# Attention scores with the row maximum set in the score banks by ScalarE, in place of a row product on TensorE

## The chip, the cores and the metric

The kernel runs on one core of one Trainium2 chip. The metric is the device time of one execution in microseconds, taken as the median over runs. The profile is of one further execution.

## What is computed

Two sequences of 1024 tokens with 128 features go through one block: a conditioned layer norm, attention with 16 heads of 64 features whose queries and keys come from latents of 64, a gated residual, a second conditioned norm, and a mixture of 8 experts with a gated residual. The change is in the attention:

```
q = rope((c_q @ w_up_q.T) split in heads);  k = rope((c_kv @ w_up_k.T) split in heads)
scores = einsum('bhqd,bhkd->bhqk', q, k) * scale
attn = softmax(scores, axis=-1)
out = einsum('bhqk,bhkd->bhqd', attn, v) @ w_out.T + residual
```

Softmax takes the maximum of each query's row away from its scores before the exponential.

## The kernel before

**Tiles and loops.** Heads are taken in pairs, 8 pairs a sequence, 16 in all (p = 0 to 15). Both heads of a pair work side by side, one on partitions 0 to 63 and one on 64 to 127. A pair has 16 steps (st): two halves of 512 queries, and in each half 8 tiles of 128 keys (kt = st % 8). A step computes the scores of 128 keys against 512 queries, keys on partitions, for both heads: 128x1024 numbers in two of the four banks of `ps_s` (even steps banks 0 and 1, odd steps banks 2 and 3). Scores are needed nearly exactly, so they are made of three products of rounded parts, upper by upper, lower by upper, upper by lower (L440, L442, L444), two matmuls each, one a head. A fourth product (L446) multiplies a stationary row of ones with `neg_row`, one row that holds minus the maximum of every query, and so takes the maximum away in PSUM. Then ScalarE writes the exponential to `probs` (L697), TensorE multiplies it with the values into `ps_o` (`pv`, L456), and GpSimd adds it up for the denominators (`add`, L939).

**The maxima.** They belong to queries, and queries have to lie on partitions to be reduced. So the same scores are computed once more, roughly and the other way round, one pair ahead: `maxima` (L422) puts 128 queries against 512 keys of both heads into `ps_m`, VectorE reduces them (`reduce_max`, L1097), and `neg_max` (L1102) makes minus the maximum of half a pair's queries, 8 numbers on each of 128 partitions (`nm`). `max_rows` (L1384) turns that into rows by 8 DMAs from SBUF to SBUF, each of 128 runs of 4 bytes. There is one `ps_m` for all: each use by TensorE waits until VectorE has reduced the one before.

**The order of the work.** It is written out by hand, in groups of two steps (g = 0 to 7). In a group of pair p, TensorE issues one maxima product of pair p+1, the scores of steps 2g and 2g+1, a second maxima product, one up projection of pair p+2 (`up`, L410), and the value steps 2g-2 and 2g-1. In groups 3 and 7 it also multiplies the denominators of half a pair (L464) into bank 2 and the output of half a pair (L473) into bank 3 of `ps_s`, after waiting for the group's exponentials; this is why the scores of steps 1 and 9 wait for `den_read` and `out_added`. Each up projection takes both halves of `ps_x`: VectorE turns it (`turn`, L1079 to L1084), ScalarE takes the upper bits (`upper`, L689), VectorE the lower bits (`lower`, L1090), and the next projection waits for that last one:

```
                elif q >= 2:
                    pe.wait_ge(s["lower"], n_unit(q, u) - 1)
```

VectorE's order in a group is: at the beginning of groups 0 and 4 the addition of the outputs to x (L1153); the first reduction; `lower` of the projection of the group before; the second reduction; in groups 3 and 7 `neg_max`; `turn`; in groups 0 and 4 the reciprocals of denominators (L1139), in groups 2 and 6 the division of the latent sums by them (L1144). ScalarE's order is: in groups 0 and 4 the copy of the denominators (`den_out`, L709); `upper` (L689); the two exponentials; in groups 0 and 4 the copy of the latent sums (L704).

**SyncE's queue**, in each pair: the second half's maxima of this pair; the denominators of a half as columns (`den_cols`, L1392), after their reciprocal back to HBM as rows (`inv_rows`, L1397) and from there spread over partitions (`inv_spread`, L1402); the first half's maxima of the next pair; the same three for the other half; the weights of pair p+4 (L1374). SyncE waits in this order, so each waits for those ahead.

The last pair has no maxima and no projections beside it, pair 14 no projections. There VectorE also normalises the first sequence and routes its tokens. Before the pairs come norms, latents and the maxima of pair 0, after them the experts.

## Time and profile before

| | |
|---|---|
| median of 3 runs | 900.91 us (897.12 to 901.8) |
| profiled execution | 895.69 us |
| its span, first to last instruction | 894.0 us |
| mean granted TensorE clock | 0.963 of full speed |
| TensorE matmuls busy | 813.2 us (91%), 5118 instructions |
| TensorE weight loads busy | 485.9 us (54%) |
| VectorE busy | 637.1 us (71%) |
| GpSimd busy | 662.7 us (74%) |
| ScalarE busy | 397.2 us (44%) |
| time on the chain that ended last | PE 82%, DVE 8%, DMA 4%, POOL 2% |

PE is TensorE's matmuls and PEld its weight loads, which run beside them; DVE is VectorE, ACT ScalarE, POOL GpSimd, SP SyncE. A matmul's recorded duration holds its way through the array, so neighbouring ones overlap: a busy share says that something was in flight, not that the engine could take no more. L numbers are lines of the kernel before. The chain of waits is followed back from the last instruction, at each step to what released it, or to the instruction before it on its engine.

### The profile page before, as it was taken

What the parts mean: (1) busy time and instruction counts of PE and PEld (TensorE: products, weight loads), DVE (VectorE), ACT (ScalarE), POOL (GpSimd) and SP (SyncE); (2) the same over time, 40 slices, a digit from 0 to 9 for tenths busy, and PEclk for the clock granted to TensorE, in tenths of its full rate; (3) what the DMA queues carried; (4) which work ended last, traced back from release to release, by engine and by line L of the source; (5) the groups of instructions that cost most, each with busy time, mean ns of one, the idle gap of its engine ahead of it and who ended that gap; (6) DMA issues with size and microseconds to landing.
All of it is one profiled execution on the core that took longest, in us unless ns stands there. A gap on an engine that the chain in (4) does not pass through costs nothing.

```text
span 894.0 us, 14690 instructions
## 1 busy us (share of the span) xinstructions
PE 813.2 (91%) x5118; PEld 485.9 (54%) x5118; DVE 637.1 (71%) x1156; ACT 397.2 (44%) x650; POOL 662.7 (74%) x348
## 2 busy tenths in 40 slices
PE   4689999999999999999999999999999977968581
PEld 2445555555555555555555555555555444368581
DVE  8987777777777777777777777777776757646022
ACT  3654444444444444444444444444444433336340
POOL 2579998898987878787878787878777856632333
PEclk8979999999999999999999999999999999969796
DMA  9101001010101011111011111101010000078683
GB/s 246 31 1 14 13 14 25 14 25 13 25 13 26 13 26 14 27 20 26 6 26 25 22 25 14 24 14 14 13 13 15 12 13 1 19 238 269 213 314 89
DMA packets 84330, 43.91 MB, mean 49 GB/s; under 512 B 57632, under 2 KB 73376, under 8 KB 84192
## 3 DMA queue, kind: packets, MB, share of 16 engines
q1 hardware_dynamic: 83232, 40.86, 18.2%
q0 software_dynamic: 1024, 2.10, 0.7%
q8 instruction: 42, 0.69, 0.3%
q14 instruction: 32, 0.26, 0.1%
HBM read 36.51 MB, written 6.16 MB: 48 GB/s over the span
## 4 chain that ended last, share of the span: by engine, by line
PE 82%; DVE 8%; DMA 4%; POOL 2%; issue 2%; ACT 1%; POOLq 0%; SPq 0%; DVEq 0%
PE ps_o L456 25%; PE ps_m L422 9%; PE ps_x L410 8%; PE ps_s L440 7%; PE ps_s L442 6%; PE ps_s L446 6%; PE ps_s L444 6%; PE ps_s L473 3%; DMA moe<-xs_dram 3%; PE ps_s L464 3%; PE ps_s L595 2%; PE ps_s L586 2%; POOL xs_dram L953 2%; DVE mx L1097 1%; PE ps_s L377 1%
## 5 line engine op out<-in xcount | busy, mean ns | idle before, releaser
L939 POOL TENSOR_TENSOR acc<-acc,probs 128x1024 f32<-128x1024 f32 (+1 forms) x192 | 459.9, 2395 | 74.7 <-ACT probs L697 52.5
L1097 DVE TENSOR_REDUCE mx<-ps_m 128x2 f32<-128x1024 f32 x240 | 293.7, 1224 | 90.9 <-PE ps_m L422 90.3
L697 ACT ACTIVATE probs<-ps_s 128x1024 f32<-128x1024 f32 x256 | 248.8, 1024 | 157.7 <-PE ps_s L446 157.6
L456 PE MATMUL ps_o<-probs,c_all 128*64 128x512 f32 x1024 | 249.5, 608 | 0.0
L440 PE MATMUL ps_s<-q_hi,k_hi 64*128 64x512 f32 x512 | 102.6, 397 | 12.0 <-DVE x_sb L1153 12.0
L456 PEld LDWEIGHTS ps_o<-probs,c_all 128*64 128x64 f32 x1024 | 62.4, 136 | 93.2 <-issue 44.5
L422 PE MATMUL ps_m<-k_hi,q_hi 64*128 64x512 f32 x480 | 107.7, 444 | 4.0 <-DVE mx L1097 4.0
L939 POOL TENSOR_TENSOR acc<-probs 128x1024 f32<-128x1024 f32 (+1 forms) x32 | 75.4, 2357 | 48.3 <-ACT probs L697 47.8
L442 PE MATMUL ps_s<-q_hi,k_lo 64*128 64x512 f32 x512 | 101.4, 391 | 0.0
L446 PE MATMUL ps_s<-neg_row,one_row 64*128 64x512 f32 x512 | 101.3, 391 | 0.0
L444 PE MATMUL ps_s<-q_lo,k_hi 64*128 64x512 f32 x512 | 100.8, 389 | 0.0
L422 PEld LDWEIGHTS ps_m<-k_hi,q_hi 64*128 64x128 f32 x480 | 46.0, 183 | 91.4 <-issue 81.3
L440 PEld LDWEIGHTS ps_s<-q_hi,k_hi 64*128 64x128 f32 x512 | 48.7, 186 | 24.0 <-issue 17.0
L1153 DVE TENSOR_TENSOR x_sb<-x_sb,ps_s 128x512 f32<-128x512 f32 x30 | 20.6, 685 | 49.9 <-PE ps_s L473 49.9
L444 PEld LDWEIGHTS ps_s<-q_lo,k_hi 64*128 64x128 f32 x512 | 48.7, 186 | 10.8
L446 PEld LDWEIGHTS ps_s<-neg_row,one_row 64*128 64x128 f32 x512 | 48.6, 185 | 10.8
L442 PEld LDWEIGHTS ps_s<-q_hi,k_lo 64*128 64x128 f32 x512 | 48.7, 186 | 10.5
L709 ACT COPY den<-ps_s 128x512 f32<-128x512 f32 x30 | 17.6, 585 | 77.9 <-PE ps_s L464 77.9
L1084 DVE TENSOR_TENSOR ps_x<-ps_x,tmp 128x256 f32<-128x256 f32 x112 | 48.4, 433 | 3.8
L689 ACT CAST q_hi<-ps_x 128x256 fp32r<-128x256 f32 x56 | 20.9, 374 | 66.8 <-DVE ps_x L1084 66.8
L1079 DVE TENSOR_TENSOR ps_x<-ps_x,rot 128x256 f32<-128x256 f32 x112 | 47.3, 422 | 0.0
L1082 DVE TENSOR_TENSOR tmp<-ps_x,rot 128x256 f32<-128x256 f32 (+1 forms) x113 | 47.1, 417 | 0.0
(299 smaller groups left out, 1025.5 us busy)
## 6 DMA issues: line engine op xcount, KB each, us to landing
probs<-in_experts SPq DMA_DIRECT2D x15, 578.0 KB, 6.0
rr<-rd_dram SPq DMA_DIRECT2D x62, 128.0 KB, 3.1
wu<-in_wqk SPq DMA_DIRECT2D x16, 256.0 KB, 3.4
neg_row<-nm SPq DMA_DIRECT2D x256, 0.5 KB, 2.0
w_first<-in_experts SPq DMA_DIRECT2D x5, 578.0 KB, 5.2
rot<-in_experts SPq DMA_DIRECT2D x5, 578.0 KB, 5.0
hT<-in_experts SPq DMA_DIRECT2D x5, 578.0 KB, 5.6
xs_dram<-zero SPq DMA_DIRECT2D x2, 960.0 KB, 9.4
```

What stands on the lines that cost most here:

```text
L410: ins = nc.tensor.matmul(bank, m[:, q % 2, w, twin, :], src, start=(n == 0), stop=(n == 1))
L422: ins = nc.tensor.matmul(bank[:, h, :], q_hi[rows(h), q % 3, qt * P:(qt + 1) * P], k_hi[rows(h), q % 3, kh * HALF:(kh + 1) * HALF], start= ...
L440: nc.tensor.matmul(bank[h], k_hi[rows(h), p % 3, kc], q_hi[rows(h), p % 3, qc], start=True, stop=False)
L442: nc.tensor.matmul(bank[h], k_lo[rows(h), p % 3, kc], q_hi[rows(h), p % 3, qc], start=False, stop=False)
L444: nc.tensor.matmul(bank[h], k_hi[rows(h), p % 3, kc], q_lo[rows(h), p % 3, qc], start=False, stop=False)
L446: ins = nc.tensor.matmul(bank[h], one_row[rows(h), :], neg_row[rows(h), p % 2, qc], start=False, stop=True)
L456: ins = nc.tensor.matmul(ps_o[64 * h:64 * h + 64, :], c_all[:, (p // HP) * TB + kt, :], probs[:, st % 4, h, :], start=(kt == 0), stop=(kt ...
L697: nc.scalar.activation(probs[:, st % 4, :, :], ps_s[:, 2 * (st % 2):2 * (st % 2) + 2, :], ACT.Exp, scale=SCALE).then_inc(s["probs"], 1)
L939: V.tensor_tensor(acc[:, half, heads, :], first, probs[:, st % 4, heads, :], ALU.add).then_inc(s["added"], 1)
L1079: V.tensor_tensor(straight, straight, cos_sb[:, c], ALU.mult).then_inc(s["turned"], 1)
L1084: V.tensor_tensor(straight, straight, part, ALU.add).then_inc(s["rotated"], 1)
L1097: V.reduce_max(mx[:, :, kh, qt], max_banks(q, n), AX.X).then_inc(s["max_reduced"], 1)
```

## The change

ScalarE copies minus the maxima, which now lie on all 128 partitions (`neg_wide`), into a step's two score banks before the scores come (`preset`), and TensorE adds the three products to what the banks hold. The fourth product, its row of ones and its row of maxima are gone. The score matmuls wait for `preset` alone. What they waited for before (the exponentials of the step two back, the maxima's landing, `den_read` and `out_added`) `preset` now waits for on ScalarE; at steps 1 and 9 it works in two pieces, bank 2 after `den_read`, bank 3 after `out_added`. In ScalarE's order the presets of the next two steps come behind the exponentials of a group, those of steps 1 and 9 behind `den_out`. The matmuls of `outputs` form one accumulation group over their bank instead of four. On TensorE value step 2g-1 moves behind the denominators and outputs.

The maxima go from `nm` to HBM by one DMA a half pair, 1024 runs of 4 bytes, and from there by two DMAs (one a head, 256 KB each) to all partitions; the two stages wait for each other. In SyncE's order they come last in each half pair, behind the inverses. The buffer is single: the spread waits until the last preset of the same half of the pair before has read it.

```
-        one_row = sb("one_row", [P, P], F32R)
-        neg_row = sb("neg_row", [P, 2, S], F32R)
+        neg_wide = sb("neg_wide", [P, 2, 2, HALF])
...
-        nm = sb("nm", [P, 2, 2, 4], F32R)
+        nm = sb("nm", [P, 2, 2, 4])
...
+        mr_dram = nc.dram_tensor("mr_dram", [2, 2, HALF], F32, kind="Internal").ap()
...
@@ -428,22 +430,15 @@
                 half, kt = divmod(st, TB)
                 if st == 0:
                     pe.wait_ge(*lowers(p))
-                ge(pe, s["probs"], n_step(p, st) - 2)
-                if kt == 0:
-                    pe.wait_ge(row_placed[half], 128 * (p + 1))
-                if kt == 1:
-                    ge(pe, s["den_read"], n_part(p, half) - 2)
-                    ge(pe, s["out_added"], n_part(p, half) - 3)
+                pe.wait_ge(s["preset"], n_step(p, st))
                 kc, qc = slice(kt * P, (kt + 1) * P), slice(half * HALF, (half + 1) * HALF)
                 bank = [ps_s[:, 2 * (st % 2) + h, :] for h in range(2)]
                 for h in range(2):
-                    nc.tensor.matmul(bank[h], k_hi[rows(h), p % 3, kc], q_hi[rows(h), p % 3, qc], start=True, stop=False)
+                    nc.tensor.matmul(bank[h], k_hi[rows(h), p % 3, kc], q_hi[rows(h), p % 3, qc], start=False, stop=False, skip_group_check=True)
                 for h in range(2):
-                    nc.tensor.matmul(bank[h], k_lo[rows(h), p % 3, kc], q_hi[rows(h), p % 3, qc], start=False, stop=False)
+                    nc.tensor.matmul(bank[h], k_lo[rows(h), p % 3, kc], q_hi[rows(h), p % 3, qc], start=False, stop=False, skip_group_check=True)
                 for h in range(2):
-                    nc.tensor.matmul(bank[h], k_hi[rows(h), p % 3, kc], q_lo[rows(h), p % 3, qc], start=False, stop=False)
-                for h in range(2):
-                    ins = nc.tensor.matmul(bank[h], one_row[rows(h), :], neg_row[rows(h), p % 2, qc], start=False, stop=True)
+                    ins = nc.tensor.matmul(bank[h], k_hi[rows(h), p % 3, kc], q_lo[rows(h), p % 3, qc], start=False, stop=True, skip_group_check=True)
                 ins.then_inc(s["scores"], 1)
...
-                                           g_all[:, p // HP, p % HP, :], start=True, stop=True)
+                                           g_all[:, p // HP, p % HP, :], start=(n == 0), stop=(n == 3))
...
-                    for n in (2 * g - 2, 2 * g - 1):
+                    def value_step(n):
                         if n >= 0:
                             pv(p, n)
                         elif p > 0:
                             pv(p - 1, NSTEP + n)
+
+                    value_step(2 * g - 2)
                     if g in (3, 7):
                         pe.wait_ge(s["probs"], n_step(p, 2 * g + 1))
                     if g == 3 and p > 0:
@@ -564,6 +561,7 @@
                         outputs(p - 1, 0, ps_s[:, 3, :])
                     if g == 7 and p > 0:
                         outputs(p - 1, 1, ps_s[:, 3, :])
+                    value_step(2 * g - 1)
...
+
+            def preset(p, st):
+
+                half, kt = divmod(st, TB)
+                if p == 0 and st < 2:
+                    act.wait_ge(s["max_reduced"], NMAX - 1 + st)
+                ge(act, s["probs"], n_step(p, st) - 2)
+                if kt == 0:
+                    act.wait_ge(row_wide[half], 32 * (p + 1))
+                if kt == 1 and (p or half):
+                    ge(act, s["den_read"], n_part(p, half) - 2)
+                    nc.scalar.copy(ps_s[:, 2, :], neg_wide[:, half, 0, :])
+                    ge(act, s["out_added"], n_part(p, half) - 3)
+                    nc.scalar.copy(ps_s[:, 3, :], neg_wide[:, half, 1, :]).then_inc(s["preset"], 1)
+                else:
+                    nc.scalar.copy(ps_s[:, 2 * (st % 2):2 * (st % 2) + 2, :], neg_wide[:, half, :, :]).then_inc(s["preset"], 1)
...
+            preset(0, 0)
+            preset(0, 1)
             for p in range(NPAIR):
                 for g in range(NGRP):
                     if g == 0 and p > 0:
                         den_out(p - 1, 0, ps_s[:, 2, :])
+                        preset(p, 1)
                     if g == 4 and p > 0:
                         den_out(p - 1, 1, ps_s[:, 2, :])
+                    if g == 4:
+                        preset(p, 9)
                     if g == 6 and p == LAST:
...
                     expo(p, 2 * g)
                     expo(p, 2 * g + 1)
+                    if g < NGRP - 1:
+                        preset(p, 2 * g + 2)
+                        if g != 3:
+                            preset(p, 2 * g + 3)
+                    elif p < LAST:
+                        preset(p + 1, 0)
...
-            V.memset(ones[:], 1.0)
-            V.memset(one_row[:].bitcast(F32), 0.0)
-            then(V.memset(neg_row[:].bitcast(F32), 0.0))
-            V.memset(one_row[0:1, :].bitcast(F32), 1.0)
-            V.memset(one_row[64:65, :].bitcast(F32), 1.0).then_inc(s["constants"], 1)
+            V.memset(ones[:], 1.0).then_inc(s["constants"], 1)
...
             def neg_max(q, half):
                 dve.wait_ge(s["max_reduced"], NMAX * q + TB * (half + 1))
-                ge(dve, row_placed[half], 128 * q)
+                ge(dve, row_out[half], 16 * q)
...
             def max_rows(q, half):
 
                 sp.wait_ge(s["max_row"], 2 * q + half + 1)
-                if q >= 2:
-                    sp.wait_ge(s["scores"], n_step(q - 2, TB * half + TB - 1))
+                sp.dma_start(mr_dram[half].rearrange("h (t p) -> p h t", p=P), nm[:, half, :, :],
+                             allow_slow_non_contiguous=True).then_inc(row_out[half], 16)
+
+            def max_spread(q, half):
+
+                sp.wait_ge(row_out[half], 16 * (q + 1))
+                if q:
+                    sp.wait_ge(s["preset"], n_step(q - 1, TB * half + TB - 1))
                 for h in range(2):
-                    for n in range(4):
-                        row = neg_row[64 * h:64 * h + 1, q % 2, half * HALF + n * P:half * HALF + (n + 1) * P]
-                        sp.dma_start(row.bitcast(F32), nm[:, half, h, n:n + 1].bitcast(F32)).then_inc(row_placed[half], 16)
+                    sp.dma_start(neg_wide[:, half, h, :],
+                                 mr_dram[half, h:h + 1, :].to_broadcast([P, HALF])).then_inc(row_wide[half], 16)
...
-            sp.wait_ge(s["constants"], 1)
-            max_rows(0, 0)
-            max_rows(0, 1)
+            for half in range(2):
+                max_rows(0, half)
+                max_spread(0, half)
             weights(3)
 
             for p in range(NPAIR):
                 if p > 0:
-                    if p < LAST + 1:
-                        max_rows(p, 1)
                     den_cols(p - 1, 0)
                     inv_rows(p - 1, 0)
                     inv_spread(p - 1, 0)
-                if p < LAST:
-                    max_rows(p + 1, 0)
+                    max_rows(p, 1)
+                    max_spread(p, 1)
                 if p > 0:
                     den_cols(p - 1, 1)
                     inv_rows(p - 1, 1)
                     inv_spread(p - 1, 1)
+                if p < LAST:
+                    max_rows(p + 1, 0)
+                    max_spread(p + 1, 0)
                 if p + 4 <= LAST:
                     weights(p + 4)
```

## Rows read from the trace of the kernel before

**Rows 1.** Busy time by stretch: stretch, its length, then each engine's busy us, TensorE's clock, DMA.

```profile
65.30:680.10 614.80, 614.01 (x3892) 349.79 (x3892) 472.20 (x777) 285.57 (x391) 523.59 (x232) 1.00 0.11 18
680.10:722.90 42.80, 39.95 (x251) 21.03 (x250) 32.71 (x45) 17.99 (x20) 34.55 (x16) 1.00 0.08 14
```

**Rows 2.** Chain of waits, 65.3 to 680.1: shares by line, then one piece.

```profile
by line: PE ps_o L456 33.7%; PE ps_m L422 12.1%; PE ps_x L410 12.1%; PE ps_s L440 8.4%; PE ps_s L442 8.4%; PE ps_s L446 8.4%; PE ps_s L444 8.3%; PE ps_s L473 4.6%; PE ps_s L464 3.8%; DVE mx L1097 0.2%; issue 0.0%
...
317.92 1.87 PE ps_o L456 x8
```

**Rows 3.** Timeline of weight loads, 314.6 to 327: start, length, and idle time before.

```profile
314.69 0.19 PEld L422 LDWEIGHTS ps_m<-k_hi,q_hi 64*128 64x128 f32 x2 [0.81 <-issue]
...
317.18 0.19 PEld L410 LDWEIGHTS ps_x<-cq,wh 128*128 128x128 f32 x1 [0.35 <-DVE q_lo L1090]
...
319.72 0.19 PEld L422 LDWEIGHTS ps_m<-k_hi,q_hi 64*128 64x128 f32 x2 [0.81 <-issue]
...
326.69 0.19 PEld L422 LDWEIGHTS ps_m<-k_hi,q_hi 64*128 64x128 f32 x2
```

**Rows 4.** Timeline of VectorE, 314.7 to 327.5.

```profile
315.24 1.23 DVE L1097 TENSOR_REDUCE mx<-ps_m 128x2 f32<-128x1024 f32 x1 [0.61 <-PE ps_m L422]
316.38 0.41 DVE L1090 TENSOR_TENSOR q_lo<-ps_x,q_hi 128x256 fp32r<-128x256 f32 x1
...
319.56 0.68 DVE L1144 TENSOR_TENSOR ou<-ou,rr 128x512 f32<-128x512 f32 x1
...
327.40 1.22 DVE L1097 TENSOR_REDUCE mx<-ps_m 128x2 f32<-128x1024 f32 x1
```

**Rows 5.** Timelines of VectorE and weight loads where TensorE waits, near 113.

```profile
112.70 0.41 DVE L1090 TENSOR_TENSOR k_lo<-ps_x,k_hi 128x256 fp32r<-128x256 f32 x1
...
113.36 0.19 PEld L410 LDWEIGHTS ps_x<-ck,wh 128*128 128x128 f32 x1 [0.24 <-DVE k_lo L1090]
```

**Rows 6.** ScalarE: timeline, and one group of instructions with busy us and mean ns.

```profile
314.66 0.37 ACT L689 CAST q_hi<-ps_x 128x256 fp32r<-128x256 f32 x1 [1.61 <-DVE ps_x L1084]
316.17 1.94 ACT L697 ACTIVATE probs<-ps_s 128x1024 f32<-128x1024 f32 x2 [1.14 <-PE ps_s L446]
...
325.72 0.58 ACT L709 COPY den<-ps_s 128x512 f32<-128x512 f32 x1 [2.59 <-PE ps_s L464]
...
L727 ACT CAST q_hi<-acc 128x512 fp32r<-128x512 f32 x1 | 0.6, 617 | 0.0
```

**Rows 7.** Timelines of GpSimd's additions and VectorE's divisions.

```profile
317.27 2.37 POOL L939 TENSOR_TENSOR acc<-acc,probs 128x1024 f32<-128x1024 f32 x1
...
319.78 2.72 POOL L939 TENSOR_TENSOR acc<-acc,probs 128x1024 f32<-128x1024 f32 x1
...
692.11 2.37 POOL L939 TENSOR_TENSOR acc<-acc,probs 128x1024 f32<-128x1024 f32 x1
...
692.62 2.41 DVE L1144 TENSOR_TENSOR ou<-ou,rr 128x512 f32<-128x512 f32 x1
```

**Rows 8.** SyncE: timeline; then DMA issues: count, size of one, median us to landing.

```profile
323.78 5.23 SPq L1384 DMA_DIRECT2D neg_row<-nm  x8
...
rr<-rd_dram SPq DMA_DIRECT2D x62, 128.0 KB, 3.1
...
xs_dram<-zero SPq DMA_DIRECT2D x2, 960.0 KB, 9.4
...
denc<-den SPq DMA_DIRECT2D x62, 2.0 KB, 2.1
...
rd_dram<-rc SPq DMA_DIRECT2D x31, 4.0 KB, 2.1
```

**Rows 9.** Timeline of ScalarE, before the first pair and in the last.

```profile
64.14 1.28 ACT L697 ACT_TABLE_LOAD   x1
...
741.82 1.94 ACT L697 ACTIVATE probs<-ps_s 128x1024 f32<-128x1024 f32 x2 [1.61 <-PE ps_s L446]
745.75 1.95 ACT L697 ACTIVATE probs<-ps_s 128x1024 f32<-128x1024 f32 x2 [1.99 <-PE ps_s L446]
```

More of the change, by code:

```diff
@@ L211, in build @@
             "max_row": "both heads' maxima of half the queries, negated (vector)",
-            "scores": "both heads' scores of a step, less the maximum (tensor)",
+            "preset": "a step's score banks hold minus the maximum (scalar)",
+            "scores": "both heads' scores of a step, added to it (tensor)",
             "probs": "their probabilities (scalar)",
@@ L250, in build @@
         up_in = sem("up_in")
-        row_placed = [sem(f"row_placed{n}") for n in range(2)]
+        row_out = [sem(f"row_out{n}") for n in range(2)]
+        row_wide = [sem(f"row_wide{n}") for n in range(2)]
         den_cols_in, inv_out, inv_in = sem("den_cols_in"), sem("inv_out"), sem("inv_in")
```

## The prediction

> **What bounds the kernel now.** I read the stretches first: 614.8 of the span's 894 us are one regular stage, from 65.3 to 680.1 us, with TensorE busy for 614.0 us at full granted clock, VectorE 472, GpSimd 524 and ScalarE 286 [rows 1]. Then the chain of waits over that stage: it names TensorE for 99.8%, and the row product (L446) for 8.4%, which is 51.6 us, or 0.23 for each of 224 steps [rows 2]. So the ready answer is that a row product taken away shortens the kernel by its own time. Before believing it I asked how late the next engine is, and laid out one group of two steps: TensorE's weight loads, which tell when it was let go [rows 3], beside VectorE's instructions of the same 5 us [rows 4]. The reader should see a loop in them. A group starts with the loads for its first maxima at 314.69. VectorE reduces that product from 315.24 (0.55 later, 1.23 long), then takes a lower half from 316.38 to 316.79, and only then may TensorE start the next up projection, which goes into the bank that this instruction read: 317.18. Projection and two value steps last until the next group's start at 319.72. These stations are in series, whatever the scores between them cost. The loop's only slack is from 316.79 to 317.18, 0.39 us, less the handover itself. How long a handover takes is shown where TensorE really waits: lower half ends 112.70+0.41=113.11, load at 113.36, so 0.25 [rows 5]. Slack: 0.14 us of a group of 5.03. The forecast rests on that number, which neither chain nor busy shares show.
>
> **The change, part by part.**
> Row product: TensorE has 0.46 us less a group, 51.6 over 14 pairs of 8 groups. Off the path comes less. The new group is 0.55 + 1.14 (315.24 to 316.38) + 0.41 + 0.25 = 2.35 to the projection, + 2.54 (317.18 to 319.72) = 4.89, against 5.03: 0.14. The other 0.32 turns into waits of TensorE for the first reduction, ahead of its second maxima, and for the lower half. The granted clock should stay: pair 14, where TensorE is busy 39.95 of 42.8 us, has it at 1.00 [rows 1].
> The Trainium skill, Trainium Kernel Development and Optimization, "Performance Expectations", calls matmul busy time a bad measure of an engine's distance to its limit and weight-load busy time a good one. By that rule TensorE, with loads for 350 us of the 615, would not be the bound and its product worth nothing; by the busy row it would be worth all; the loop lies between, nearer to the rule.
> Groups with denominators and outputs last 326.69-319.72=6.97, 1.94 more [rows 3]. One value step (half of 1.87 [rows 2]) now stands behind the outputs: nothing is added, but VectorE adds the outputs 0.9 us earlier against the next group, where it had held up the reduction (327.40 is 0.71 behind the start, not 0.55 [rows 4]), 0.02 beyond the slack. A half pair was 3 x 5.03 + 6.97 + 0.02 = 22.08 and becomes 4 x 4.89 + 1.94 = 21.50: 0.58 less.
> VectorE's division, once a half pair behind the third group's rotation, waits for GpSimd's addition to end: issued at 319.56, done at 320.24, the addition ending at 317.27+2.37=319.64 [rows 4, 7]. Its end was just in time for the next reduction, due 0.55 behind 319.72. GpSimd takes 2.51 from one addition to the next (317.27 to 319.78), 5.02 a group, more than 4.89: released 2.35 behind the second group (0.23 earlier than now, with the scores), three in a row end at 9.78, that is 4.89 behind the third. The division ends 0.60 later at 5.49, the reduction was due at 4.89+0.55=5.44, and it needs 0.02 more to start: between 0.07 and, with a lengthened addition, 0.11. I take 0.11. Net 0.47 a half pair. Pairs 1 to 13: 26 x 0.47 = 12.2; pair 0, without divisions, 7 x 0.14 = 1.0.
> Presets: 256 copies of 128x1024 new on ScalarE. No row copies from SBUF to PSUM. Below: an Exp of this shape, two in 1.94, so 1.02 alone and 0.92 in a row; above: the SBUF-sourced cast of half the size, 0.617, doubled to 1.23 [rows 6]. I take 1.02/0.92, the row with the same size. ScalarE's group is then 0.37 (upper half) + 1.94 + 1.84 = 4.15, with the upper bound 4.77: under 4.89, so TensorE's group hides it. In time: exponentials ran from 1.48 to 3.42 behind the group's start, now 0.23 earlier, to 3.2; presets end at 4.1 and 5.0, wanted by scores at 5.0 and 5.7. Were that cover gone, each 0.1 us more a preset would cost 0.2 a group.
> At a half pair ScalarE has the denominators' copy (0.58), one bank's preset, a wait for VectorE's output addition, the other bank's preset, and queued behind that wait an upper half and the next exponentials. Outputs are ready 2.35+2.54+1.94-0.94=5.9 behind the fourth group's start, added at 6.85, preset at 7.5; TensorE wants the bank at 7.65 and has 0.3 of idle time above. Zero, with 0.4 of cover.
> Maxima's way: SyncE had 8 small DMAs a half pair (5.2 us of issuing [rows 8]) ahead of the inverses; now 1+2 behind them. From the denominators: two DMAs 2.1+0.6, reciprocal in VectorE's turn (done 5.1 behind the pair's start), inverse rows 2.1, two spreads issued in 1.2, maxima to HBM X, spread of twice the size 1.2+3.7 (3.1 for half of it) [rows 8]: 13.3+X, wanted by the ninth preset at 17.8, harmless until 19.8 by the cover above. X: 2.1 for the inverse rows' write of 256 runs, below; 9.4 for the zero fill's 1920 runs of 512 B, above. I take 3, nearest to the write of small runs. Zero. The weight DMA queued behind has a pair's time; the other half's rows go the same way four groups later.
> Start: two presets and the table load of 1.28, idle time until now [rows 9], get in front of the first exponentials: +0.8. The memsets gone at the beginning lay beside the token DMAs: 0. Pair 14 has no projections and waits for reductions already; earlier output additions: -0.4. Last pair: groups of 3.93 (741.82 to 745.75 [rows 9]) meet ScalarE's 1.94+1.84+0.25=4.03: +0.5; its long waits for VectorE's router stay.
> Sum: -12.2-1.0+0.8-0.4+0.5 = -12.3. The profiled execution took 895.7 (1.7 of it round the span), so 883.4; the shown runs' median is 5.2 above it, so **888.6** for that median.
>
> **Rivals.**
> B, the product was on the path with all its time: 900.9-51.6-0.4=849. For: chain and busy time [rows 1, 2]. Against: 0.25 us of handover [rows 5]; it would have to vanish, and reductions to move with it.
> C, slower: the division falls behind the next addition instead of ahead of it. Where it met a running one it took 2.41, not 0.68: 692.62+2.41=695.03, 0.55 after that addition's end at 694.48 [rows 7]. It decides if GpSimd starts the next addition (5.03 behind the group) before the division is issued (4.75 to 4.87), a margin of 0.2. Then the division ends at 8.0 and the reduction is 2.5 late, 26 times: 900.9-12.3-2.9+65=951. The Trainium skill, SBUF — State Buffer, "Who interferes with whom", makes it a rule: a VectorE instruction with two SBUF inputs and a GpSimd one that reads SBUF exclude each other, and the first to start keeps the ports; by that rule, the trace agrees (2.41 against 0.68).
> D, rows late: 1024 runs of 4 bytes need X above 6.5. At the far bound of 9.4: 2.9 x 26 = 75 more, 900.9-12.3+75=964; break-even at X=7.0. Against: the 256 runs' 2.1. The Trainium skill, DMA: Bandwidth & Descriptors, speaks against such a write in "Rules for kernel authors" (a strided last dimension becomes one descriptor per element) and "Specifications" (below 512 B an engine reads, modifies and writes); it gives no time, and no run here shows such a write to HBM.
> E, ScalarE in the way: presets at 1.23 and the wait for output additions cost half a microsecond a half pair and eat the gain of 12: 898 to 903.
>
> **How the numbers follow.** The forecast's mechanism 0.70, B 0.07, C 0.08, D 0.04, E 0.11. Its own range is 880 to 896: 0.06 of a handover times 112 (7), with runs 5 apart. 8 in 10 lie between 868 (handovers 0.1 cheaper, 11, no delay by divisions, 3, and a fast run) and 904 (E); B is left below, C and D above. Within 0.5% (896.4 to 905.4) is about what a measurement of this kernel cannot tell from no change. Faster: 0.69+0.07=0.76; same: E and the forecast's edge, 0.12; slower: C and D, 0.12.
>
> **What would show it.** Groups of 4.89 between loads for first maxima; TensorE waiting some 0.3 us a group for reductions and lower halves, 112 times, and no longer busy all the stage; divisions still near 0.7; presets near 1.02, the ninth not waiting for rows. Groups of 4.57 mean B, divisions of 2 to 3 us C, a half pair's first preset behind a DMA D, scores waiting for presets E.

## Result: slower by 8%, and the profile after

The changed kernel takes **974.03 us** (median of 4 runs, 967.99 to 986.77) against 899.01 for the kernel before beside it: ratio 1.081, interval 1.074 to 1.088; the ratio leaves out the run of 986.77, a slow one with a granted clock of 0.915 against 0.924 to 0.938. The forecast was 888.6 in a range of 868 to 904. It fell into rival D, rows late, to which I had given 0.04 and a time of 964.

The page of the kernel after, its busy times, its chain, two groups of instructions:

```profile
span 972.6 us, 13807 instructions
...
PE 829.1 (85%) x4606; PEld 451.4 (46%) x4606; DVE 642.9 (66%) x1152; ACT 634.8 (65%) x937; POOL 662.5 (68%) x348
...
DMA 51%; PE 17%; DVE 15%; issue 6%; ACT 5%; SPq 4%; POOL 1%; ACTq 0%; POOLq 0%; DVEq 0%
...
L712 ACT COPY ps_s<-neg_wide 128x1024 f32<-128x1024 f32 x225 | 222.4, 1026 | 136.8 <-DMA neg_wide<-mr_dram 136.8
```

Over its whole span the chain of the kernel before was 82% TensorE's and 4% DMA's (in the regular stage 99.8% TensorE's [rows 2]); the chain of this one is 51% DMA's. The presets last 1.03 us, as bounded, but ScalarE idles 136.8 us ahead of them, for the maxima's rows. The chain of waits of one half pair (start, length, what) shows where these are; SPq is SyncE's queue:

```profile
307.98 7.56 DMA mr_dram<-nm
...
315.94 4.66 DMA neg_wide<-mr_dram
...
320.68 0.04 ACT ps_s L712
```

The write of 1024 neighbouring runs of 4 bytes takes 7.56 us here. Over the whole execution, from the summary of that one line (L1400), it takes from issue to landing:

```profile
DMA to landing us min/median/max: 7.6/9.1/10.3
```

The timelines of ScalarE and of weight loads around it (start, length, the engine's instruction, and in brackets its idle time before):

```profile
320.68 1.02 ACT L712 COPY ps_s<-neg_wide 128x1024 f32<-128x1024 f32 x1 [3.22 <-DMA neg_wide<-mr_dram]
```

```profile
309.40 0.19 PEld L424 LDWEIGHTS ps_m<-k_hi,q_hi 64*128 64x128 f32 x2 [0.81 <-issue]
...
311.75 0.19 PEld L412 LDWEIGHTS ps_x<-cq,wh 128*128 128x128 f32 x1 [0.25 <-DVE k_lo L1111]
...
314.28 0.19 PEld L424 LDWEIGHTS ps_m<-k_hi,q_hi 64*128 64x128 f32 x2 [0.81 <-issue]
```

ScalarE waits 3.22 us for one preset. The half pair with this wait in it, from the outputs at 319.17 to those at 341.76, is 22.59 us long, 0.97 more than the 21.62 of a version without such waits (e13 below); the one ahead of it, with a wait of 4.20, is 23.58, 1.96 more. So some 2.2 us of each wait are covered, near the 2.0 of the forecast. The one behind them, with a wait of 4.26, is 25.16, 3.54 more: over it TensorE is granted 0.93 of its clock, over the other two 1.00. The mean over all half pairs is 24.8. And a group that doesn't meet this wait answers to [rows 3] exactly as forecast: 314.28 - 309.40 = 4.88 us between first maxima, the projection 2.35 behind the start, and TensorE waiting for the lower half with a handover of 0.25. So two things were to be shown: that this write alone cost the time, and that the rest does bring what the loop said.

### The profile page after: what moved, and what is told of

It is laid out like the page before. It is cut to its first block, busy times and chain, and to the rows that moved or that the text cites. A ratio compares the mean times of both kernels' runs of the same rounds, so it can differ in the third digit from the quotient of the medians.

```text
span 972.6 us, 13807 instructions
## 1 busy us (share of the span) xinstructions
PE 829.1 (85%) x4606; PEld 451.4 (46%) x4606; DVE 642.9 (66%) x1152; ACT 634.8 (65%) x937; POOL 662.5 (68%) x348
## 3 DMA queue, kind: packets, MB, share of 16 engines
q0 software_dynamic: 1024, 2.10, 0.7%
## 4 chain that ended last, share of the span: by engine, by line
DMA 51%; PE 17%; DVE 15%; issue 6%; ACT 5%; SPq 4%; POOL 1%; ACTq 0%; POOLq 0%; DVEq 0%
DMA mr_dram<-nm 27%; DMA neg_wide<-mr_dram 12%; DMA rd_dram<-rc 8%; DVE mx L1118 4%; SPq L1428 3%; PE ps_s L437 3%; PE ps_o L451 2%; PE ps_s L441 2%; PE ps_m L424 2%; PE ps_s L439 2%; DMA moe<-xs_dram 2%; ACT ps_s L710 2%; PE ps_s L584 1%; PE ps_s L593 1%; ACT ps_s L712 1%
## 5 line engine op out<-in xcount | busy, mean ns | idle before, releaser
L712 ACT COPY ps_s<-neg_wide 128x1024 f32<-128x1024 f32 x225 | 222.4, 1026 | 136.8 <-DMA neg_wide<-mr_dram 136.8
L695 ACT ACTIVATE probs<-ps_s 128x1024 f32<-128x1024 f32 x256 | 250.4, 1024 | 61.7 <-PE ps_s L441 61.3
L451 PE MATMUL ps_o<-probs,c_all 128*64 128x512 f32 x1024 | 263.2, 625 | 0.0
L437 PE MATMUL ps_s<-q_hi,k_hi 64*128 64x512 f32 x512 | 114.9, 443 | 67.6 <-ACT ps_s L712 43.2
L424 PE MATMUL ps_m<-k_hi,q_hi 64*128 64x512 f32 x480 | 120.4, 492 | 12.3 <-DVE mx L1118 9.6
L441 PE MATMUL ps_s<-q_lo,k_hi 64*128 64x512 f32 x512 | 107.6, 412 | 0.0
L439 PE MATMUL ps_s<-q_hi,k_lo 64*128 64x512 f32 x512 | 107.4, 412 | 0.0
L441 PEld LDWEIGHTS ps_s<-q_lo,k_hi 64*128 64x128 f32 x512 | 52.4, 198 | 11.7
L1111 DVE TENSOR_TENSOR q_lo<-ps_x,q_hi 128x256 fp32r<-128x256 f32 x56 | 23.3, 416 | 28.4 <-ACT q_hi L687 28.3
L468 PEld LDWEIGHTS ps_s<-hT,ou 128*128 128x128 f32 x240 | 29.0, 191 | 24.5 <-issue 23.5
L412 PE MATMUL ps_x<-ck,wh 128*128 128x256 f32 x112 | 39.4, 370 | 0.0
L1111 DVE TENSOR_TENSOR k_lo<-ps_x,k_hi 128x256 fp32r<-128x256 f32 x56 | 23.3, 417 | 24.0 <-ACT k_hi L687 24.0
```

The lines of the kernel that those rows point to most:

```text
L424: ins = nc.tensor.matmul(bank[:, h, :], q_hi[rows(h), q % 3, qt * P:(qt + 1) * P], k_hi[rows(h), q % 3, kh * HALF:(kh + 1) * HALF], start= ...
L437: nc.tensor.matmul(bank[h], k_hi[rows(h), p % 3, kc], q_hi[rows(h), p % 3, qc], start=False, stop=False, skip_group_check=True)
L439: nc.tensor.matmul(bank[h], k_lo[rows(h), p % 3, kc], q_hi[rows(h), p % 3, qc], start=False, stop=False, skip_group_check=True)
L441: ins = nc.tensor.matmul(bank[h], k_hi[rows(h), p % 3, kc], q_lo[rows(h), p % 3, qc], start=False, stop=True, skip_group_check=True)
L451: ins = nc.tensor.matmul(ps_o[64 * h:64 * h + 64, :], c_all[:, (p // HP) * TB + kt, :], probs[:, st % 4, h, :], start=(kt == 0), stop=(kt ...
L695: nc.scalar.activation(probs[:, st % 4, :, :], ps_s[:, 2 * (st % 2):2 * (st % 2) + 2, :], ACT.Exp, scale=SCALE).then_inc(s["probs"], 1)
```

## Experiments

**Two ways to make the write harmless, first try.** One writes runs of 16 bytes and turns them round in the preset's read:

```diff
-mr_dram[half].rearrange("h (t p) -> p h t", p=P), nm[:, half, :, :]
+mr_dram[half].rearrange("h (p t) -> p h t", p=P), nm[:, half, :, :]
...
-nc.scalar.copy(ps_s[:, 2, :], neg_wide[:, half, 0, :])
+nc.scalar.copy(ps_s[:, 2, :].rearrange("q (t p) -> q t p", p=P), neg_wide[:, half, 0, :].rearrange("q (p t) -> q t p", p=P))
...
```

The copies of the other presets are turned the same way.

> After, with the maxima written to HBM as 256 runs of 16 bytes instead of 1024 of 4; the preset's copy reads them in turned order. Theory W (the write of 1024 short runs, 9.1 us median, is what made the change slower; all else of the forecast holds): the write lands in 2.2 to 2.9 like the inverse rows' 256 runs, the ninth and first presets no longer wait for their rows, groups stay 4.89, half pairs fall from about 25 to 21.6, the time is 885 to 892. Rival S (the two stages through HBM, with 256 KB spreads last in SyncE's queue, are too long as such): the write is short but presets still wait over 1 us a half pair; 900 to 930. Rival A (ScalarE, with 640 us of work and its waits, is the limit): waits move to TensorE for presets; 900 or more. A preset over 1.1 us would mean that the turned read costs.

Measured: 1005.7 us, ratio 1.121 (1.117 to 1.125). The write lands 2.9 us after its issue (median), no preset waits for rows, and yet it is slower still:

```profile
L712 ACT COPY ps_s<-neg_wide 128x1024 f32<-128x1024 f32 x225 | 454.3, 2065 | 0.0
...
L695 ACT ACTIVATE probs<-ps_s 128x1024 f32<-128x1024 f32 x256 | 253.9, 1056 | 4.1 <-PE ps_s L441 3.5
```

A copy that reads every fourth word takes 2.07 us instead of 1.03, and ScalarE, idle 0 and 4.1 us ahead of its two large groups, has become the bound. The run shows that the write can be had cheaply; what the rest of the change is worth it could not show.

The other keeps the 4-byte runs and issues the write first in a half pair's DMAs, its spread last:

```diff
 if p > 0:
+    max_rows(p, 1)
     den_cols(p - 1, 0)
     inv_rows(p - 1, 0)
     inv_spread(p - 1, 0)
-    max_rows(p, 1)
     max_spread(p, 1)
+if p < LAST:
+    max_rows(p + 1, 0)
...
```

> After, with 1024 runs of 4 bytes kept, but the write issued first in each half pair and only its spread last. Theory W with the DMA engines' rings in common: the write still takes 7 to 9 us, but lands before the spread is due; if the small denominators' DMAs issued behind it land in 2 us as ever, the time is that of the 16-byte version, 885 to 892. If they have to wait behind it (landing in 5 us or more), VectorE stands at its reciprocal at the end of groups 0 and 4, and the time lies between, 900 to 950. Rival S: no gain against after, about 974, since the spread is last all the same.

Measured: 965.7 us (one run), 8 less than the change and above the 900 to 950 expected. The presets' wait for rows is gone but for 4.4 us in all. One of the waits of the whole run (what waits for what, us in all, times, the longest) shows where it went:

```profile
DVE rc L1160 <- DMA denc<-den: 78.0, 29, 5.5
```

The reciprocals wait for the denominators' small DMAs, which had landed in 2.1 us [rows 8] and now stand behind the slow write in SyncE's queue: issued at 312.12, 1.70 us behind a write, they let the reciprocal start at 319.83. A slow write is not hidden by being issued early, if short DMAs that are wanted soon come behind it. (What the rest of the 965.7 is made of was not followed up.)

**The loop alone: the kernel before without its row product.** No maxima are subtracted, and the exponentials' scale is small so that they stay finite; all else is left.

```diff
-for h in range(2):
-    ins = nc.tensor.matmul(bank[h], one_row[rows(h), :], neg_row[rows(h), p % 2, qc], start=False, stop=True)
```

> Before, with the row product left out and nothing in its place: maxima aren't subtracted (the exponential's scale is made small so that it stays finite), rows are still made and moved. TensorE's work falls by 51.6 us. Loop theory (projection, value steps, first reduction and lower half in series, 0.14 us of slack a group): 5.03 a group becomes 4.89 in three groups of four, nothing in the groups behind outputs, where VectorE adds outputs first, less what divisions that end late take: 8 to 13 us less, 886 to 892. Rival B (the product was on the path with all of its time): 50 less, 848.

Measured: 885.5 us, ratio 0.988 (0.985 to 0.992), 11.7 us for 51.6 us of TensorE's work. Its weight loads:

```profile
308.33 0.18 PEld L422 LDWEIGHTS ps_m<-k_hi,q_hi 64*128 64x128 f32 x2 [0.81 <-issue]
...
310.68 0.19 PEld L410 LDWEIGHTS ps_x<-cq,wh 128*128 128x128 f32 x1 [0.25 <-DVE q_lo L1088]
...
313.21 0.18 PEld L422 LDWEIGHTS ps_m<-k_hi,q_hi 64*128 64x128 f32 x2 [0.81 <-issue]
```

A group of 4.88. **And the other way: the product twice.**

```diff
+for h in range(2):
+    nc.tensor.matmul(bank[h], one_row[rows(h), :], neg_row[rows(h), p % 2, qc], start=True, stop=True)
```

> Before, with the row product computed twice a step (the first time overwritten, so the output is the same). Loop theory: TensorE at 5.03 is the limit from here upwards, so 0.46 a group count in full where TensorE was without pause: 45 to 52 us more, 942 to 950, although taking one away gave only 12. If work on TensorE counted alike in both directions, it would be 12 more, 909.

Measured: 952.0 us (one run), 54.7 above the kernel before. Its loads for first maxima:

```profile
307.47 0.19 PEld L422 LDWEIGHTS ps_m<-k_hi,q_hi 64*128 64x128 f32 x2 [0.81 <-issue]
...
312.95 0.19 PEld L422 LDWEIGHTS ps_m<-k_hi,q_hi 64*128 64x128 f32 x2 [0.81 <-issue]
```

5.48. Groups are 4.88, 5.03 and 5.48 for none, one and two row products: the first one added costs 0.15 of its 0.46, the next one 0.45. That is the kink at which one bound hands over to another, and the kernel before stood 0.15 us from it.

**The write by itself.** Behind the end of the kernel before, twelve DMAs, one at a time, each waited for; six kinds, twice. The time of the whole says nothing here.

```diff
+tried(o_near[0].rearrange("h (t p) -> p h t", p=P), ...)            # 1024 x 4 B, neighbours, HBM
+tried(o_far[:, :, 0:1], ...)                                       # 1024 x 4 B, each in its own 512 B
+tried(o_near[1].rearrange("h (p t) -> p h t", p=P), ...)            # 256 x 16 B, neighbours
+tried(o_mid.rearrange("r p c -> p r c"), ...)                       # 1024 x 16 B
+tried(flat_rt[:, 0:16:2], ...)                                     # 1024 x 4 B to SBUF
+tried(o_near[0].rearrange("h (t p) -> p h t", p=P)[:, :, 0:1], ...) # 256 x 4 B, neighbours
```

> Before, with six DMAs behind its end, twice over, each waited for alone: 1024 runs of 4 bytes to HBM, the runs side by side (4 KB in all); 1024 runs of 4 bytes to HBM, each in its own 512 bytes; 256 runs of 16 bytes, side by side; 1024 runs of 16 bytes, side by side; 1024 runs of 4 bytes to SBUF; 256 runs of 4 bytes, side by side. The time of the kernel is 30 to 60 us longer and isn't the point. In after the 1024 packets had all moved 3.3 us after the issue and the landing was told only at 7.6. Theory N (neighbours in one line of HBM are written one after the other): alone 1024 runs take 7.5 to 9 side by side, but under 4 apart, and 3 to 4 to SBUF; 16-byte runs, a quarter as many in a line, take 2.5 and 1024 of them under 5. Theory C (each short run to HBM costs, wherever it lies): apart as long as side by side, 7.5 to 9; 1024 runs of 16 bytes as long too; 256 runs of 4 bytes as long as 256 of 16. To SBUF 3 to 4 by both.

Measured, SyncE's timeline: each DMA starts when the one above has landed.

```profile
895.65 0.37 SPq L1511 DMA_DIRECT2D o_near<-den  x1
904.45 0.63 SPq L1511 DMA_DIRECT2D o_far<-ou  x1
909.00 0.37 SPq L1511 DMA_DIRECT2D o_near<-rr  x1
910.56 0.36 SPq L1511 DMA_DIRECT2D o_mid<-tmp  x1
913.97 0.66 SPq L1511 DMA_DIRECT2D rt_sb<-acc  x1
916.32 0.36 SPq L1511 DMA_DIRECT2D o_near<-rot  x1
924.16 0.36 SPq L1511 DMA_DIRECT2D o_near<-den  x1
934.12 0.55 SPq L1511 DMA_DIRECT2D o_far<-ou  x1
938.01 0.36 SPq L1511 DMA_DIRECT2D o_near<-rr  x1
```

1024 neighbours of 4 bytes take 8.80 and 9.96 us. The same 1024, each in its own 512 bytes of HBM: 4.55 and 3.89. A quarter of them, still neighbours: 7.84. 256 runs of 16 bytes: 1.56; 1024 of 16 bytes: 3.41; 1024 of 4 bytes to SBUF: 2.35. So among 4-byte neighbours the number of runs hardly matters (8.80 against 7.84 for a quarter), while that they lie side by side in HBM and are of 4 bytes does. In both slow cases 128 runs share each stretch of 512 bytes, so 7.8 to 10 us would be 61 to 78 ns a run if such a stretch takes its runs one after another: an inference, which no run here sees directly. The rows don't tell how long a stretch would be; with a shorter one fewer runs share it, and each would take longer. The Trainium skill, DMA: Bandwidth & Descriptors, "Why small descriptors are slow (HBM only)", says that SBUF to SBUF is spared; 2.35 against 8.80 agrees, though its two mechanisms, fixed costs of each descriptor, would not tell near from far.

**Plain presets with 16-byte runs.** For these the tile of maxima must hold every fourth query, as its stationary side (the wait for the queries' projections is widened to match):

```diff
-q_hi[rows(h), q % 3, qt * P:(qt + 1) * P],
+q_hi[rows(h), q % 3, qt // 4 * HALF + qt % 4:(qt // 4 + 1) * HALF:4],
```

> After, with 256 runs of 16 bytes and the preset's plain read: the maxima's tiles take every fourth query of a half (a stationary operand with a step of 16 bytes), so that each partition's four maxima are neighbours. Against the 16-byte version before, in which the write landed in 2.9 us but the preset, reading with a step of 16 bytes, took 2.07 us instead of 1.03. Theory W (the short-run write alone made the change slower): write 2 to 3 us, presets 1.03, no preset waits for rows, groups 4.89, half pairs 21.5 to 21.7, time 882 to 889, that is 10 to 15 less than the kernel before. Rival A (ScalarE, or presets as such, cost even when plain): 895 or more with TensorE waiting for presets. Rival L (weight loads with a step are slow): loads for maxima well over 0.19 us and groups above 4.9.

Measured: 913.2 us, ratio 1.017 (1.012 to 1.022); 92 us less than e1, 61 less than the change. No wait for rows, presets at 1029 ns. What is left over the forecast is in the weight loads, by group and in the timeline:

```profile
L424 PEld LDWEIGHTS ps_m<-k_hi,q_hi 64*128 64x128 f32 x480 | 77.7, 306 | 151.2 <-issue 151.1
```

```profile
318.26 0.31 PEld L424 LDWEIGHTS ps_m<-k_hi,q_hi 64*128 64x128 f32 x2 [0.81 <-issue]
...
323.38 0.31 PEld L424 LDWEIGHTS ps_m<-k_hi,q_hi 64*128 64x128 f32 x2 [0.81 <-issue]
```

A load with a step of 16 bytes takes 306 ns, not 183, and both maxima of a group stand in the loop: 5.12 us a group. (The up projection starts behind the slower loads of the second maxima and no longer waits for the lower half.) 112 groups of 0.24 more are 27 us, which is what e6 takes over the last version below. The Trainium skill, SBUF — State Buffer, "Door 1: The DMA port swizzle", has a note on SBUF's lines of 16 bytes: each access that crosses to a new line pays a penalty. Words 16 bytes apart cross at every access. e1's copy (2.07 against 1.03) and this load agree.

**Two orders of the value steps, on top of e6.** First, both steps ahead of denominators and outputs, as before the change:

```diff
                     value_step(2 * g - 2)
+                    value_step(2 * g - 1)
...
-                    value_step(2 * g - 1)
```

> The version with every fourth query, but both value steps ahead of denominators and outputs as in the kernel before. The forecast gave the move almost nothing on the reduction (0.02 a half pair) but the cover for the preset of steps 1 and 9: without it the output addition ends about 0.9 us later against the next group, its preset at 1.6 instead of 0.7 behind the group's start, where TensorE wants the bank at 0.8 and has 0.4 of idle time: 0.4 to 0.7 a half pair, 10 to 18 us slower than with the move. If the move is worth nothing, the two are within 3 us.

Measured: 910.6 us, ratio 1.013 (1.008 to 1.019), 3 less than e6 where 10 to 18 more had been expected: a miss. What the move was to shield does come onto the chain, in each half pair, and is on none of e6's: the outputs' addition and the preset behind it.

```profile
313.05 0.70 DVE x_sb L1174
...
313.77 0.60 ACT ps_s L710
```

But TensorE has the next group's first maxima and first scores to do meanwhile, and the value steps, together again, take 1.87 us instead of twice 1.01. Half pairs are 22.5 us here and 22.6 in e6: the move gives back what it brings. Second, one value step ahead of the second maxima, to fill TensorE's wait, and the division behind the fourth group's lower half:

```diff
+                    value_step(2 * g - 2)
                     if p < LAST:
                         maxima(p + 1, 2 * g + 1)
...
+                    if p > 0 and g in (3, 7):
+                        divide(p - 1, g // 4)
```

> The version with every fourth query, and the loop opened: value step 2g-2 goes between the scores and the second maxima product, so that TensorE has work while VectorE reduces and makes the lower half; the division goes behind the lower half of groups 3 and 7, since behind the rotation, which now ends later, it would fall into GpSimd's next addition. Loop theory: TensorE's own 4.57 plus 0.2 for one more change between matmul kinds, 4.77 a group instead of 4.89, 112 times: 8 to 14 us below the version with every fourth query, 870 to 878. Rival (VectorE or ScalarE is the limit just as well, or the division is blocked anyway): same or slower than that version.

Measured: 920.0 us, ratio 1.025 (1.020 to 1.030), 7 slower than e6 and not 8 to 14 faster: a miss too. VectorE waits 178 us for maxima, 131 in e6, but TensorE does not wait for it any more: none of its up projections waits for a lower half, and from 80 to 660 us all pieces of the chain are TensorE's own. Most of one group of it:

```profile
318.86 1.01 PE ps_o L451 x4
319.86 0.56 PE ps_m L424 x2
320.42 0.67 PE ps_x L412 x4
321.09 1.01 PE ps_o L451 x4
```

With six score pieces of 0.23 that is 5.19 us a group, e6's being 5.12. The loop was opened as meant; TensorE's own time, expected at 4.77, was mis-sized. Against the 4.57 that it started from, value steps apart take 2.02 instead of 1.87, first maxima with their stepped loads 0.56 instead of 0.43, and second maxima, stepped and now behind a value step, 0.56 instead of the 0.23 of plain ones behind scores in the kernel before: 0.61 in all. A step moved into a wait gains only if parting it from its like costs less than the wait, some 0.3 us a group by the prediction's working. The moved division is in the same run and wasn't tried apart; no piece of the chain is its.

**Steps on the moving side instead.** Maxima and presets are plain; the score products read queries with a step, and the outputs' product takes every fourth column:

```diff
-q_hi[rows(h), p % 3, qc], start=False
+q_hi[rows(h), p % 3, qc].rearrange("r (t p) -> r p t", p=P), start=False
-ou[:, half, n * P:(n + 1) * P],
+ou[:, half, n:HALF:4],
```

> The changed kernel with the maxima written as 256 runs of 16 bytes, as in e1 and e6, but with plain maxima tiles and a plain preset read: the three products of a score step read their moving queries with a step of 128 words inside groups of four, so that the banks' columns have the order of the rows, and the product of the outputs, four loads a half pair, takes every fourth column back as its stationary side. The softmax and the values don't care for the order of the queries. Theory (only the row write and e6's slow loads were in the way, and a moving operand's step costs nothing): the write lands in about 3 us, presets take 1.03, the ninth doesn't wait for rows, weight loads for maxima are back at 183 ns, a group is 4.89 again instead of e6's 5.12, and a half pair 4 x 4.89 + 1.94 = 21.5, plus four stepped loads of 0.12 more each beside products: 885 to 897, ratio 0.985 to 0.998. Rival 1 (moving queries with a step are read slower): score products of 128x512 rise from 0.39 to 0.78 or more; 16 steps of 6 in a pair: 14 x 16 x 6 x 0.39 = 524 us more, near 1400; at a tenth of that rise, 950. Rival 2 (the stepped load of outputs is on the path with its 0.12 each and more): 28 x 0.5 = 14 more, 899.

Measured: 911.9 us, ratio 1.013 (1.011 to 1.016). Groups by form:

```profile
L437 PE MATMUL ps_s<-q_hi,k_hi 64*128 64x512 f32 x512 | 116.2, 450 | 12.0 <-ACT ps_s L710 11.5 <-ACT ps_s L712 0.5
...
L468 PE MATMUL ps_s<-hT,ou 128*128 128x128 f32 x240 | 64.0, 410 | 0.1
...
L468 PEld LDWEIGHTS ps_s<-hT,ou 128*128 128x128 f32 x240 | 58.3, 327 | 24.5 <-issue 23.5 <-ACT probs L695 1.0
```

And its chain, the outputs of one half pair:

```profile
172.29 2.06 PE ps_s L468 x8
```

The score products rose from 0.39 to 0.45 us, and the loop's idle time took it (groups without outputs are still 4.88 or 4.89). But outputs are in series with everything: 2.06 on the chain instead of 1.09, once a half pair, 28 x 0.97 = 27 us. Rival 2, with twice the price I had put on it. Half pairs are 22.6.

**No step anywhere.** The rows are turned round by the DMAs, in three hops of which none writes 4-byte neighbours to HBM (the first writes 128 of 32 bytes), and the hops stand between the steps of the inverses in SyncE's queue:

```diff
+sp.dma_start(mc_dram[half].rearrange("p (h t) -> p h t", h=2), nm[:, half, :, :])                       # 128 x 32 B to HBM
+sp.dma_start(one.rearrange("o (j p) -> o j p", p=P), mc_dram[half:half + 1].rearrange("o p j -> o j p")) # 4 B reads, to one row of SBUF
+sp.dma_start(mr_dram[half:half + 1].rearrange("o h n -> o (h n)"), one)                                 # one run of 4 KB
-sp.dma_start(mr_dram[half].rearrange("h (t p) -> p h t", p=P), nm[:, half, :, :])
```

> The changed kernel with plain maxima tiles, plain presets and plain score products; only the way of the maxima to the wide tile is another: 128 runs of 32 bytes to HBM, a read of it in 4-byte elements into one row of SBUF, that row to HBM in one run, and the spread as before. The three hops stand in SyncE's queue between the steps of the inverses, the first of them ahead, so that each flies while another is waited for. Theory (the loop through VectorE sets 4.89 a group; of the change only the write of 4-byte neighbours to HBM is wrong): no small DMA above some 4 us, no preset waits for rows, groups of 4.88 to 4.90, half pairs near 21.6, 884 to 892, ratio 0.982 to 0.993; the first such version that is faster than both. Rival 1 (4-byte neighbours are slow in SBUF too, when one partition takes all of them): the second hop lands 8 us or more after its issue, small DMAs behind it wait as in e2, 930 to 965. Rival 2 (no write is slow, but SyncE's queue with three more DMAs a half pair makes the division's inverses late): the division waits for its rows by a microsecond or more a half pair, 900 to 930. Rival 3 (something else in the changed kernel holds the half pair at 22.6, as in e6 and e11): groups of 4.89 but half pairs of 22.6, 910.

Measured: **886.6 us** (885.42 to 890.22), ratio 0.989 (0.986 to 0.992): faster than both kernels. Weight loads, from one half pair's outputs to the next one's:

```profile
299.45 0.97 PEld L470 LDWEIGHTS ps_s<-hT,ou 128*128 128x128 f32 x8 [0.81 <-issue]
...
311.31 0.18 PEld L426 LDWEIGHTS ps_m<-k_hi,q_hi 64*128 64x128 f32 x2 [0.81 <-issue]
...
316.19 0.19 PEld L426 LDWEIGHTS ps_m<-k_hi,q_hi 64*128 64x128 f32 x2 [0.81 <-issue]
...
321.07 0.97 PEld L470 LDWEIGHTS ps_s<-hT,ou 128*128 128x128 f32 x8 [0.81 <-issue]
...
323.17 0.19 PEld L426 LDWEIGHTS ps_m<-k_hi,q_hi 64*128 64x128 f32 x2 [0.81 <-issue]
```

VectorE, the division and the reduction behind it, and the presets' group:

```profile
316.03 0.73 DVE L1167 TENSOR_TENSOR ou<-ou,rr 128x512 f32<-128x512 f32 x1
316.74 1.23 DVE L1120 TENSOR_REDUCE mx<-ps_m 128x2 f32<-128x1024 f32 x1
```

```profile
L714 ACT COPY ps_s<-neg_wide 128x1024 f32<-128x1024 f32 x225 | 222.9, 1030 | 3.4 <-DMA neg_wide<-mr_dram 3.4
```

321.07 - 299.45 = 21.62 us a half pair; the waits for rows are 3.4 us in all. Of its stage from 64 to 673 us TensorE is busy for 601 of 609 by the table of stretches:

```profile
64.00:673.00 609.00, 601.45 (x3466) 310.88 (x3466) 478.24 (x781) 500.83 (x648) 521.95 (x232) 1.00 0.18 43
```

So even here, where its up projection waits for VectorE's lower half in 98 of 112 groups, the busy row would still name TensorE.

## Why the prediction was wrong, and where it was right

**The step that failed** is one term of the sum: X, the write of the maxima's rows, "I take 3, nearest to the write of small runs". It measured 9.1 (7.6 to 10.3). That this is near the far bound of 9.4 is chance: that row moves 960 KB in runs of 512 bytes and says nothing of short ones. The row that I had called nearest writes 256 runs of 16 bytes. I matched small with small and count with count; what decided was the size of a run against its neighbours in HBM, which no row of before varied. With both ends on the table, 2.1 and 9.4, and the break-even between them at 6.5 to 7.0, a chance of 0.04 for D was no reading of the rows: only a value near the lower end was safe.

Everything else on that path was sized rightly. "13.3+X": in the chain above, from the denominators' issue at 299.64 to the rows at 320.60 are 20.96, of which the write has 7.56, so 13.4. The cover was near 2.0, as seen above. Rival D's price, "2.9 x 26", "964": at 974 the change is 87 us slower than e13, 3.1 for each of 28 half pairs; D's mechanism holds, its price came close partly by chance. What D left out is TensorE's clock, of which the prediction says that it "should stay": in this stage TensorE, waiting more, was granted 0.95 of it against 1.00 [rows 1]. Between 176 and 521 us, the seven half pairs granted 1.00 are longer than 21.62 by their wait less 1.9 to 2.3; the three single ones granted 0.93 are so by another 1.5, the two granted 0.88 by another 2.6 and 1.6. Taken over the stage, an estimate from these rows, some 20 of the 87 us go with the lower clock, and D with the measured 9.1, 2.6 x 26 = 68, gives the rest. No run here has the waits without it.

```profile
65.30:757.00 691.70, 633.49 (x3450) 321.75 (x3450) 480.38 (x778) 495.79 (x644) 521.51 (x231) 0.95 0.18 38
```

**The loop** was right. Group forecast 4.89, measured 4.88 in the change, in e4 and in e13; projection forecast 2.35 behind the start, measured 2.35 (311.75 - 309.40); handover 0.25, measured 0.25. Half pair before 22.08 in the working, and it is 22.07 in the trace; forecast 21.50 + 0.11, measured 21.62 in e13. Two parts of that are wrong and cancel. The division's delay of 0.11 isn't there: it ends at 316.76, the reduction starts 0.55 behind the group's start, as without it. And the fourth group is 6.98, not 4.89 + 1.94 = 6.83: two value steps in two places stand as 1.01 twice in e13's chain, where together they were 1.87 [rows 2].

```profile
319.27 1.01 PE ps_o L453 x4
320.28 0.86 PE ps_s L461 x4
321.14 1.09 PE ps_s L470 x8
322.23 1.01 PE ps_o L453 x4
```

**The sum**, -12.3, stands against -10.8 for e13 and -11.7 for e4. The small terms (start +0.8, last pairs -0.4 and +0.5) were not tried one by one.

**B** (all of the product's time) is refuted by e4. **C** didn't occur: the median division is 0.73 or 0.74 in the change and in e13; a single one of 2.6 and 2.5 has its like in the 2.41 of the kernel before [rows 7]. **E**: presets are 1.03, not 1.23. In all of e13 TensorE's score products wait 15.5 us for presets behind added outputs, in three waits, and 3.4 us for others; in the kernel before they waited 12.0 us, in three, for the additions themselves. The moved value step, which I had counted as adding nothing, adds those 0.15 a half pair and shields about as much: e7 without the move is no slower than e6.

## What to carry to other kernels

Before work is taken off a busy engine, find the loop through the other engines and its slack: a bound 0.14 us away caps the gain, whatever the busy share and the chain say (here 12 of 52 us); and doubling the same work shows the kink in one more run. When a change puts a transfer on a path with a break-even between the two bounds of its price, its chance belongs to how far the nearest row differs in kind (run length, neighbours, destination), not to its nearness in size. A permutation cost time wherever it was read or written with a step on a serial path: 1.0 us a preset on ScalarE, 0.12 us a weight load, 6 us a write; as hops of DMAs that each stay cheap it was free.

## What was not expected of the hardware

Besides the times of small writes above: the slow write is not slow in moving packets. In the table of DMA traffic of the kernel after, the first line is from 308.6 to 311.4 us, the second from 311.4 to 315.5:

```profile
DMA packets 1158, 0.21 MB, mean 74 GB/s; under 512 B 1066, under 2 KB 1066, under 8 KB 1157
...
DMA packets 0, 0.00 MB, mean 0 GB/s; under 512 B 0, under 2 KB 0, under 8 KB 0
```

These are more than the write's 1024 runs, none are left after 311.4, and the write landed at 315.54: for 4.1 us no packet moved, and SyncE still waited. A queue's busy share does not show such a write; only issue to landing does. What goes on in these 4 us no run shows.
